# Layer one's running mean: the division by the token count moves from VectorE behind the running sums into ScalarE's scales

## The reference, cut to what matters

```
avg = cumsum(x, axis=1) / arange(1, l + 1)            # per batch and channel
ci  = avg, head by head                               # [b*H, l, 16]
pc  = ci @ W_pe + b_pe                                # [b*H, l, 62]
dyn, gate = pc[..., :31], pc[..., 31:]
energy = stt_energy + sigmoid(gate) * dyn
w   = softmax(energy, axis=-1), masked at the start
out = sum over 31 taps of w[:, :, k] * ci shifted by k
v   = out @ W_fc.T + x
return layernorm(v) * gamma + beta
```

## Time and profile before

| | us |
|---|---|
| median of 3 runs | 3478.79 |
| lowest, highest | 3476.23, 3479.75 |
| profiled execution, its span | 3478.2 |

### The profile page before, as it was taken

The page is one execution under the profiler, slowest core; times in us unless marked ns, Lnnn a source line. Parts: engine busy times, 40 slices in busy tenths (PEclk is TensorE's granted clock), DMA queues, the critical chain, the costliest instruction groups (busy, mean ns, idle before and its releaser), DMA issues.

```text
span 3478.2 us, 67597 instructions
## 1 busy us (share of the span) xinstructions
PE 3312.0 (95%) x25168; PEld 2784.9 (80%) x25168; DVE 2655.0 (76%) x6172; ACT 2077.6 (60%) x4055; POOL 1267.5 (36%) x1073
## 2 busy tenths in 40 slices
PE   7999999999996899999999469999999999999999
PEld 4888888888885789999999447888888888888888
DVE  5888888888877865555555488888888888888884
ACT  4677767776764556556655345555555555555554
POOL 1333333333331276666665333333233322323320
PEclk9999999999998999999999789999999999999999
DMA  5323332222212254444444365555655556555641
GB/s 179 101 85 104 109 112 82 89 81 80 73 34 92 67 124 93 107 107 105 95 106 94 69 136 106 126 128 125 127 127 119 124 125 129 129 124 127 129 102 41
DMA packets 746021, 366.38 MB, mean 105 GB/s; under 512 B 551278, under 2 KB 696246, under 8 KB 745558
## 3 DMA queue, kind: packets, MB, share of 16 engines
q1 hardware_dynamic: 717278, 319.57, 36.2%
q0 software_dynamic: 28416, 42.49, 6.6%
HBM read 224.93 MB, written 135.99 MB: 104 GB/s over the span
## 4 chain that ended last, share of the span: by engine, by line
PE 82%; DVE 8%; ACT 3%; issue 2%; DMA 2%; POOL 1%; SPq 1%; POOLq 0%; ACTq 0%; DVEq 0%
PE bank L2291 10%; PE bank L1609 10%; PE bank L1593 10%; PE bank L2305 10%; PE bank L850 9%; PE bank L830 9%; PE bank L2262 7%; PE bank L130 5%; PE bank L2241 3%; PE bank L2273 3%; PE bank L807 2%; DVE x L732 2%; DVE stats L643 1%; PE bank L2236 1%; ACT sides L1137 1%
## 5 line engine op out<-in xcount | busy, mean ns | idle before, releaser
L1489 DVE TENSOR_TENSOR hidden_low<-bank,hidden_high 128x512 fp32r<-128x512 f32 x256 | 176.2, 689 | 263.1 <-ACT hidden_high L1190 263.0
L1183 ACT ACTIVATE bank<-bank,fc_bias 128x512 f32<-128x512 f32 x256 | 169.5, 662 | 263.6 <-PE bank L1593 263.6
L850 PE MATMUL bank<-w_high,gT_low 128*128 128x256 f32 x1024 | 314.8, 307 | 1.8 <-DVE gT_low L722 1.8
L606 ACT ACTIVATE bank<-bank,b 128x512 f32<-128x512 f32 x256 | 168.7, 659 | 244.7 <-PE bank L830 241.9
L2049 ACT ACTIVATE bank<-bank,l_b 128x512 f32<-128x512 f32 x256 | 168.9, 660 | 237.1 <-PE bank L2291 236.9
L2305 PE MATMUL bank<-l_w_high,l_hidden_low 128*128 128x256 f32 x1024 | 307.6, 300 | 0.0
L2262 PE MATMUL bank<-bandT,window 128*32 128x96 f32 x5632 | 270.3, 344 | 24.7 <-DMA bandT<-bands 21.4
L850 PE MATMUL bank<-w_high,gT_high 128*128 128x256 f32 x1024 | 289.7, 283 | 0.0
L850 PE MATMUL bank<-w_low,gT_high 128*128 128x256 f32 x1024 | 289.6, 283 | 0.0
L2305 PE MATMUL bank<-l_w_low,l_hidden_high 128*128 128x256 f32 x1024 | 286.0, 279 | 0.0
L2305 PE MATMUL bank<-l_w_high,l_hidden_high 128*128 128x256 f32 x1024 | 285.5, 279 | 0.0
(11 more groups left out here) (372 smaller groups left out, 10752.1 us busy)
## 6 DMA issues: line engine op xcount, KB each, us to landing
bandT<-bands SPq DMA_DIRECT2D x352, 240.0 KB, 3.7
fc_full<-in_L_ffn_fc_wT SPq DMA_DIRECT2D x32, 1024.0 KB, 5.7
bands<-zeros SPq DMA_DIRECT2D x22, 768.0 KB, 7.5
x<-in_L_attn_x SPq DMA_DIRECT2D x32, 512.0 KB, 5.9
moe_output<-zeros SPq DMA_DIRECT2D x32, 512.0 KB, 6.2
x_after_retention<-x SPq DMA_DIRECT2D x32, 512.0 KB, 3.0
moe_input_and_gates<-xn SPq DMA_DIRECT2D x32, 512.0 KB, 4.6
moe<-moe_output SPq DMA_DIRECT2D x32, 512.0 KB, 7.3
```

The source lines that it names most:

```text
L850: m = pe.matmul(out, x, w, start=False, stop=f == KF - 1 and j == 2 and c % 2 == 1)
L1183: e.activation(bank[:, :], bank[:, :], ACT.Gelu, bias=t.b1[:, x, f:f + 1]).then_inc(s("hidden_full"), 1)
L1489: v.tensor_tensor(t.hidden.low[:, n % SLICES, :], K.banks[t.bank["expand", i, f, 0]][:, :], t.hidden.high[:, n % SLICES, :], ALU.subtract) ...
```

## The change

`average` is renamed `run_sum`. The scan writes straight into the padded ring, now called `sumT`, and the multiplication by 1/(t+1) is gone, and with it the tile `sums` and VectorE's wait for itself. What follows works with sums, which are the averages times the count t+1, and is set right on ScalarE, where tokens stand on partitions so that the count is one number a partition:

- The bias row is multiplied by the count: the matmul L2236 takes a row of counts, as fp32r, where it had ones.
- Tanh has the scale 0.5/(t+1), read from a column `half_count`, where it had the number 0.5.
- `energy` is multiplied by the count, by a new instruction of ScalarE for every chunk, `e.mul` into `scaled_energy` (a ring of two). It stands in the step `kernel_product`, behind ScalarE's wait for the product and before the tanh. GpSimd adds `scaled_energy[n % 2]`, and waits for it.
- Exp has the scale 1/(t+1), a column of `per_count`, where it had none.
- The copy to `window` becomes an activation Copy with the scale 1/(t+1), a column of `per_window`.

The places of all steps stay as they are. Three loads are added before layer one, and `per_count` becomes a small one. The row of counts is loaded to `l1_h_full`, and VectorE copies it (128x1024) in `prepare`.

```diff
-    "turn_in": (9, 17.63), "average": (9.98, 10.16, 17.95, 18.16), "add_row": (11.69, 19.69),
+    "turn_in": (9, 17.63), "run_sum": (9.98, 10.16, 17.95, 18.16), "add_row": (11.69, 19.69),
...
-    t.loads = 16 * 10
+    t.loads = 16 * 13
...
             e.wait_ge(s("gated_energy"), n + 1)
-            e.tensor_tensor(e1[:, :, :], e1[:, :, :], t.energy[:, :, :], ALU.add).then_inc(s("full_energy"), 1)
+            e.wait_ge(*K.later("scaled_energy", n + 1))
+            e.tensor_tensor(e1[:, :, :], e1[:, :, :], t.scaled_energy[n % 2][:, :, :], ALU.add).then_inc(s("full_energy"), 1)
...
             e.wait_ge(s("kernel_product"), n + 1)
             if n >= 2:
                 e.wait_ge(s("gated_energy"), n - 1)
-            e.activation(t.th[n % 2][:, :, :], kernel_view(K, t, b, ch, 1), ACT.Tanh, scale=0.5).then_inc(s("gate"), 1)
+            if n >= 2:
+                e.wait_ge(s("full_energy"), n - 1)
+            e.mul(t.scaled_energy[n % 2][:, :, :], t.energy[:, :, :], t.count[:, ch:ch + 1]).then_inc(K.later("scaled_energy")[0], 1)
+            e.activation(t.th[n % 2][:, :, :], kernel_view(K, t, b, ch, 1), ACT.Tanh, scale=t.half_count[:, ch:ch + 1]).then_inc(s("gate"), 1)
...
-            e.activation(t.e[n % 2][:, :, :], t.e[n % 2][:, :, :], ACT.Exp).then_inc(s("exp"), 1)
+            e.activation(t.e[n % 2][:, :, :], t.e[n % 2][:, :, :], ACT.Exp, scale=t.per_count[:, args[0]:args[0] + 1]).then_inc(s("exp"), 1)
...
-            e.copy(out, src).then_inc(s("window"), 1)
+            e.activation(out, src, ACT.Copy, scale=t.per_window[:, args[0]:args[0] + 1]).then_inc(s("window"), 1)
...
+        v.tensor_copy(t.counts[:, :], t.counts_full)
+        v.tensor_scalar(t.half_count[:, :], t.per_count[:, :], 0.5, None, ALU.mult)
...
-        elif name == "average":
+        elif name == "run_sum":
             half, k = divmod(args[0], KD)
-            sums, tokens = t.sums[:, k, :], slice(half * BANK, (half + 1) * BANK)
+            tokens, at = slice(half * BANK, (half + 1) * BANK), PAD + half * BANK
+            sums = t.sumT[b % 2][:, k, :]
             v.wait_ge(s("h3T"), KD * (2 * b + half) + k + 1)
+            if half:
+                v.wait_ge(s("sumT"), KD * (2 * b) + k + 1)
             if b >= 2:
                 v.wait_ge(s("window_turned"), NT * (b - 1))
-            v.tensor_tensor_scan(sums, t.h3T[b % 2][:, k, tokens], K.zero[:, 0:1].to_broadcast([P, BANK]), sums[:, BANK - 1:BANK] if half else 0.0,
-                                 ALU.add, ALU.add).then_inc(step, c.up())
-            v.wait_ge(step, c.n)
-            v.tensor_tensor(t.avgT[b % 2][:, k, PAD + half * BANK:PAD + (half + 1) * BANK], sums, t.per_count[:, tokens], ALU.mult).then_inc(s("avgT"), 1)
+            v.tensor_tensor_scan(sums[:, at:at + BANK], t.h3T[b % 2][:, k, tokens], K.zero[:, 0:1].to_broadcast([P, BANK]),
+                                 sums[:, at - 1:at] if half else 0.0, ALU.add, ALU.add).then_inc(s("sumT"), 1)
...
-                pe.matmul(pair[r][:, 0:4 * t.RW], t.ones[rows, :], t.pe_bias[rows, :, :, :, :].rearrange("o a j q k -> o (a j q k)"), start=True, stop=False)
+                pe.matmul(pair[r][:, 0:4 * t.RW], t.counts[rows, ch * P:(ch + 1) * P], t.pe_bias[rows, :, :, :, :].rearrange("o a j q k -> o (a j q k)"), start=True, stop=False)
```

More of the change, by code:

```diff
@@ L1672 @@
       "add_in": (5.29, 12.04), "stats_in": (6.3, 13.26), "root_in": (7.29, 15.43), "norm_in": (7.83, 15.71), "load_bias_row": 5.68,
-      "turn_in": (8.99, 17.62), "average": (9.97, 10.15, 17.37, 18.15), "add_row": (11.83, 19.83),
+      "turn_in": (8.99, 17.62), "run_sum": (9.97, 10.15, 17.37, 18.15), "add_row": (11.83, 19.83),
       "kernel_product": (10.79, 12.87, 14.85, 16.8, 18.79, 20.8, 22.79, 24.8),
@@ L1737, in layer_one_tiles @@
     t.row_gain, t.row_bias, t.row_out = (K.tile(ctx, n, [P, D]) for n in ("row_gain", "row_bias", "row_out"))
-    t.h3T, t.avgT = K.ring(ctx, "h3T", 2, [P, KD, S]), K.ring(ctx, "avgT", 2, [P, KD, PAD + S + PAD])
-    t.sums = K.tile(ctx, "sums", [P, KD, BANK])
+    t.h3T, t.sumT = K.ring(ctx, "h3T", 2, [P, KD, S]), K.ring(ctx, "sumT", 2, [P, KD, PAD + S + PAD])
     t.convT = K.tile(ctx, "convT", [P, KD, t.CIRCLE])
@@ L1792, in layer_one_early_sync @@
                 A["L1_attn_stt_energy"].rearrange("a (j r c) b k -> (a b) r j (c k)", j=K.KD, r=2)[:, r, :, :].to_broadcast([P, K.KD, t.RW])) for r in range(2)),
-             (t.b1[:, :], A["L1_ffn_b1_c"]), (t.per_count[:, :], A["per_count"].to_broadcast([P, K.S])),
+             (t.b1[:, :], A["L1_ffn_b1_c"]), (t.per_count[:, :], A["per_count"]), (t.per_window[:, :], A["per_window"]), (t.counts_full, A["counts"].to_broadcast([P, K.S])), (t.count[:, :], A["token_counts"]),
              (t.w_pe[:, :, :, :].rearrange("p a q k -> p (a q k)"), A["w_pe_blocks"])]
@@ L1948, in layer_one_pool @@
             for i in range(2):
-                e.memset(t.avgT[i][:, :, 0:t.PAD], 0.0)
-                e.memset(t.avgT[i][:, :, t.PAD + K.S:], 0.0).then_inc(s("pool_setup"), 1)
+                e.memset(t.sumT[i][:, :, 0:t.PAD], 0.0)
+                e.memset(t.sumT[i][:, :, t.PAD + K.S:], 0.0).then_inc(s("pool_setup"), 1)
             e.memset(t.window[0][:, :, :, :], 0.0)
@@ L2231, in layer_one_tensor @@
                 pe.wait_ge(*K.setup("vector", "rows_split"))
-            pe.wait_ge(s("avgT"), KD * (2 * b + ch // HC + 1))
+            pe.wait_ge(s("sumT"), KD * (2 * b + ch // HC + 1))
             pair = [take(t.bank["kernel_product", b, ch, r], "gated_energy", n + 1) for r in range(2)]
@@ L2240, in layer_one_tensor @@
                     out = pair[r][:, 0:4 * t.RW].rearrange("p (a j c) -> p j a c", a=2, j=KD)[:, j, :, :]
-                    m = pe.matmul(out, t.avgT[b % 2][rows, j, PAD + ch * P:PAD + (ch + 1) * P],
+                    m = pe.matmul(out, t.sumT[b % 2][rows, j, PAD + ch * P:PAD + (ch + 1) * P],
                                   t.w_pe[rows, :, :, :].rearrange("p a q k -> p (a q k)"), start=False, stop=j == KD - 1)
@@ L2248, in layer_one_tensor @@
                 pe.wait_ge(*K.setup("pool", "bands"))
-            pe.wait_ge(s("avgT"), KD * (2 * b + min((i + 1) * TT - 1, K.S - 1) // BANK + 1))
+            pe.wait_ge(s("sumT"), KD * (2 * b + min((i + 1) * TT - 1, K.S - 1) // BANK + 1))
             bank = take(t.bank["window_turn", b, i, 0], "window", n + 1)
-            turn_columns(pe, bank, KD, lambda k: t.avgT[b % 2][:, k, i * TT:i * TT + P], K.ident, s("window_turned"))
+            turn_columns(pe, bank, KD, lambda k: t.sumT[b % 2][:, k, i * TT:i * TT + P], K.ident, s("window_turned"))
         elif name == "convolve":
@@ L2437 @@
     arrays["w_pe_blocks"] = arrays["w_pe_blocks"].reshape(P, -1)
-    arrays["per_count"] = (np.float32(1) / np.arange(1, S + 1, dtype=np.float32)).reshape(1, S)
+    arrays["counts"] = np.arange(1, S + 1, dtype=np.float32).reshape(1, S)
+    arrays["token_counts"] = columns(arrays["counts"])
+    arrays["per_count"] = columns(np.float32(1) / arrays["counts"])
+    taps, reach = 96, P - 96
+    tokens = taps * np.arange(-(-S // taps))[None, :] + p[:, None] - reach
+    arrays["per_window"] = np.where((tokens >= 0) & (tokens < S), np.float32(1) / np.clip(tokens + 1, 1, S).astype(np.float32), np.float32(1))
     nc = bacc.Bacc("TRN2", target_bir_lowering=False, num_devices=1)
```

9 lines of the change are left out of this document (6 added, 3 removed).

## The result

The changed kernel takes 3486.85 us (median; 3483.56 to 3490.85), the one before 3478.83 us in the same comparison (3473.88 to 3482.83). The ratio is 1.0024, 95% interval 1.0017 to 1.0031: slower by 8 us, between 6 and 11. I had forecast 3489.5 and a range of 3478 to 3498.

The account below looks back on a forecast made before the run. TensorE was taken as the bound, nine tenths or more busy behind layer one's start, so its few waits decide. 3478.2 - 2 (start) + 9.7 (l1_expand waits) + 3.5 (turn_mid) = 3489.4; stated 3489.5 us, range 3478 to 3498.

Parts of the forecast that it names:

- The first place: Once a batch l1_expand waits for a bank behind tanh and VectorE: 0.48 grows to 1.17 us, 14 x 0.69 = 9.7.
- The second place: turn_mid's transposes, once a batch taking a bank of another chunk's product: 0.25 us lost a batch, 3.5 us in all.
- my better case: At turn_mid: VectorE's shorter queue lets ScalarE's run start earlier, so only 0.15 us a batch is lost.
- my other value: At turn_mid: ScalarE's run does not start earlier and exp's 0.09 adds, so 0.44 us a batch is lost.
- The start: Beginning of layer one, where VectorE is a bound: 2 us gained, bounds 4.9 us gained to 5.5 us lost.
- The removed multiplications at nothing in a settled batch: VectorE's 64 multiplications, 44 us, lie outside the waiting chain in settled batches, so removing them gains zero there.
- the cover: VectorE's queue, 1.2 us shorter behind each removed pair of multiplications, gives slack for turn_mid's wait.
- The rival in which VectorE was the bound: Removed VectorE work shrinks the fourteen l1_expand waits (4.6 us) and the start (4.9): 3469 us, chance 0.08.
- the reading by occupancy: A skill page's rule names the engine of highest occupancy: VectorE at 87% against TensorE's weight loads at 81%.
- The sum: Whole kernel: 3478.2 - 2 + 9.7 + 3.5 = 3489.4, add 0.6 to the median; stated as 3489.5 us, 0.3% slower.
- Columns: ScalarE's scales read from columns in tanh, exp and window copy: 0.09 us each, bounds 0 and 0.13.
- the fourteen: The l1_expand waits, one a batch from 2126 to 3296 us, 0.48 us each, forecast to become 1.17.

Follow-up runs that it names:

- experiment 6: (no_columns) Changed kernel with tanh, exp and window-copy scales as before, no columns, division left out there; 3482.86 us, ratio 1.0011 to the kernel before.
- Experiments 1: (mul_early) Changed kernel with ScalarE's multiplication moved ahead of its wait for the product; 3480.47 us, ratio 0.9997 to the kernel before.
- 10: (mul_behind) Changed kernel with tanh first and ScalarE's multiplication behind it; 3476.0 us, ratio 0.9989 to the kernel before; run again 3477.0 us, 0.9994.
- experiment 5: Changed kernel with 64 second passes put back on VectorE behind the scans, values unchanged; 3493.63 us, ratio 1.0044 to the kernel before.
- Experiment 4: Kernel before with the scan straight into avgT, VectorE's multiplications left out and nothing added on ScalarE; 3480.08 us, ratio 0.9993 to the kernel before.
- run 1534: Not a run label: 1534 ns is the median duration of GpSimd's tensor_scalar over the whole run of mul_gpsimd.
- mul_gpsimd: Changed kernel with the multiplication made by GpSimd ahead of its wait and gone from ScalarE; 3561.12 us, ratio 1.0233 to the kernel before.

## Why the prediction was right

The direction, the place and the mechanism held. Step by step:

- *The first place.* Forecast 0.48 to 1.17 us and 14 x 0.69 = 9.7; measured 1.14 and 14 x 0.66 = 9.2. Spacing of the multiplication 0.61 (I had 0.60). Tanh with its column takes 0.07 us more than before; the column by itself is worth 0.09, as I had it, and the place behind the multiplication takes 0.02 off (experiment 6). Experiments 1 and 10 show by taking it away that the latency is the cause.
- *The second place* is the term that I sized too large: 0.25 us a batch, 3.5 us. The eight transposes grew by 0.10, near the 0.15 of my better case, and 0.05 is gained at the second product's bias, which I had not named. So the distance's growth beyond the first place is 0.70 - 0.66 = 0.04 us a batch, 0.6 us. I had left open whether VectorE's shorter queue would give ScalarE its idle time back. It does; without it the transposes grow by 0.36 to 0.43 in the last seven batches (experiment 5), near my other value of 0.44, but by 0.10 in the early ones. I took a value between two cases where one of them held.
- *The start.* Forecast 2 us gained, found 3.0, and 3.7 in the second trace. Experiment 4 puts the multiplications' own worth there at 3.9 us, experiment 5 at 2.6 (159.7 against 157.1; 3.3 against the second trace). So the new work costs under 1 us of it.
- *The removed multiplications at nothing in a settled batch.* Held: 0.07 us a batch (experiment 4), plus the cover. The rival in which VectorE was the bound fell with it, and with it the reading by occupancy: VectorE stood at 87%, against 81% for the weight loads, and in experiment 4 it lost 44 us of work with nothing added, for 0.07 us a batch and 3.9 us in the start. VectorE's share went to 83% (I had 84), ScalarE's to 65% (I had 66).
- *The sum.* 9.2 + 0.6 - 3.0 + 0.2 = 7.0 us in layer one, measured 8.0 with an interval of 6 to 11; I had 11.2. Of the 4.2 us too many, 2.9 lie in the second place, 1.0 in the start and 0.5 in the first place, less the 0.2 of the tail; no large error hid another. A slip stands in my sum: 3489.4 plus the 0.6 to the median is 3490.0, and I wrote 3489.5.
- *Columns.* I counted 0.09 for tanh, exp's only in the worse case of the second place, and the window's at nothing. With their growth (exp 712 against 619 ns by the medians, the window's copy 467 against 376) the columns cost 0.19 us a batch, 0.10 at the fourteen and 0.09 at `turn_mid` (experiment 6); elsewhere in a batch nothing is found. Which of the three columns the 0.09 belongs to is not settled.

What stays open: why the start of mul_behind is 2 us shorter than that of mul_early, and why layer one begins up to 8 us apart.

## What to carry to other kernels

In a kernel whose busiest engine waits almost nowhere, look up the few waits that recur and walk each back through the engines: work on such a chain costs its full latency times the count, and work off it next to nothing while there is idle time to spare behind it, whatever the engines' loads say. Small waits can hide inside a run of matmuls, where only the run's length shows them (1.03 us against 1.14 and 1.39). A new instruction that doesn't need what its engine waits for belongs behind the one that does, if its reader is late anyway: here swapping two neighbouring lines was worth 10 us. Ahead of the wait it is free only where the engine's idle time there is long enough for it. Moving a step in a list that also hands out buffers changes both; keep the hand-out fixed to learn what the order does.

## What the runs showed of the hardware

- GpSimd's tensor_scalar with a column, 128x496 fp32, took 1597 ns in the mean (median of the whole run 1534), longer than its tensor_tensor of that size with two inputs (1254 ns) and over twice ScalarE's 711 ns (mul_gpsimd, changed kernel).
- On ScalarE a column as scale added 91 ns to tanh (566 to 657 in the mean, both directly behind the multiplication; no_columns against the changed kernel), 93 to exp (medians, 619 to 712) and 91 to a copy (medians, 376 to 467; both the kernel before against the changed one).
- Tanh directly behind the multiplication was some 19 ns shorter than tanh elsewhere: without a column 566 ns (no_columns) against 585 (before), with one 657 (changed) against 676 (mul_behind). The means are of 128 each.
- The time from the program's start to layer one differed by up to 8 us (1964.3 to 1972.7) between traces of kernels whose first two stages are alike; two traces of one kernel lay 0.5 us apart (the changed kernel, 1968.0 and 1967.4) and 0.4 (mul_behind, 1964.4 and 1964.8).
